# A decoder block on one core: first projections by pairs of batches, and the call lists of all five engines reordered

## The reference, cut to what matters

```python
x = x + attn(layernorm(x))                     # 8 batches, 128 tokens, 256 wide, 16 heads of 16
x = x + long_convolution(ctx, ctx, layernorm(x))
x = x + ffn(layernorm(x))                      # 4-bit weights, 2048 wide

def attn(x):
    q, k, v = x @ Wq, x @ Wk, x @ Wv
    scores = (q . k) * tril                    # masked by a product, so masked scores are 0
    return softmax(scores / 128 ** 0.5) . v @ Wo

def long_convolution(k, v, q):                 # 16 heads of 8
    kv = k_i * v_j                             # all pairs i, j of a head, per position
    y = causal_conv(kv, ssm_kernel) + kv * D
    return sum over i of y_ij * q_i

def ffn(x):
    Wg, Wu, Wd = (LUT[code] * scale for each)  # codes of 4 bits, a scale for each 32
    return (gelu(x @ Wg.T) * (x @ Wu.T)) @ Wd.T
```

## Time and profile before

| | us |
|---|---|
| median of 3 runs | 258.29 |
| lowest and highest | 256.86, 259.73 |
| span of the profiled execution | 256.6 |
| TensorE busy | 240.9 (94%) |
| VectorE busy | 158.8 (62%) |
| GpSimd busy | 138.8 (54%) |
| ScalarE busy | 127.3 (50%) |

### The profile page before, as it was taken

How to read it: one execution, slowest core, us unless ns; L and a number is a source line. 1 busy time by engine, 2 the same in 40 slices (tenths; PEclk the granted TensorE clock), 3 DMA queues, 4 the chain that set the end, 5 groups by cost and what they waited for, 6 DMA issues and landing times.

```text
span 256.6 us, 4952 instructions
## 1 busy us (share of the span) xinstructions
PE 240.9 (94%) x1840; PEld 153.7 (60%) x1840; DVE 158.8 (62%) x287; ACT 127.3 (50%) x273; POOL 138.8 (54%) x173
## 2 busy tenths in 40 slices
PE   7999999999999998876899999999999999999993
PEld 7855776566556665554445666556566566566562
DVE  1889747777798989876689976317145182322124
ACT  2345665477587777752676254325333333523230
POOL 4257563631418969796889941273453635433230
PEclk9999999999999999997999999999999999999999
DMA  6995996932030303100030000004030000000004
GB/s 192 380 353 150 164 225 201 163 66 93 3 125 4 126 4 89 42 0 0 0 125 0 0 3 1 3 0 125 0 109 17 0 3 0 0 3 0 0 0 166
DMA packets 15104, 18.81 MB, mean 73 GB/s; under 512 B 1448, under 2 KB 12776, under 8 KB 15080
## 3 DMA queue, kind: packets, MB, share of 16 engines
q1 hardware_dynamic: 15080, 18.49, 26.5%
HBM read 15.21 MB, written 3.15 MB: 72 GB/s over the span
## 4 chain that ended last, share of the span: by engine, by line
PE 80%; DVE 9%; ACT 3%; issue 3%; DMA 2%; POOL 1%; SPq 0%; DVEq 0%; ACTq 0%; POOLq 0%
PE bank L1245 39%; PE bank L1411 16%; PE bank L1301 4%; PE bank L1299 4%; PE bank L1303 3%; PE bank L1317 3%; PE bank L1482 2%; DMA X<-in_x 2%; PE bank L1369 2%; PE bank L1480 2%; ACT PT L616 2%; PE bank L1334 1%; DVE o_sb L985 1%; DVE tail L976 1%; DVE mx L960 1%
## 5 line engine op out<-in xcount | busy, mean ns | idle before, releaser
L1034 DVE SCALAR_TENSOR_TENSOR QK<-bank,QK 128x512 f32<-128x512 f32 x32 | 22.0, 689 | 60.7 <-PE bank L1245 59.7
L464 POOL TENSOR_TENSOR QK<-QK 128x512 f16<-128x512 f32 x24 | 27.7, 1156 | 56.4 <-ACT QK L645 56.4
L655 ACT ACTIVATE QK<-bank 128x512 f32<-128x512 f32 x32 | 19.0, 595 | 60.9 <-PE bank L1245 60.8
L1245 PE MATMUL bank<-xTh,Wa 128*128 128x512 f16 x128 | 40.5, 379 | 0.6 <-DVE xTl L1059 0.6
L1245 PE MATMUL bank<-xTh,Wb 128*128 128x512 f16 x128 | 40.7, 379 | 0.0
L440 POOL TENSOR_TENSOR arena<-Ys,qx 128x640 f32<-128x640 f32 x16 | 25.5, 1592 | 4.1 <-ACT qx L698 4.1
L1245 PE MATMUL bank<-xTl,Wb 128*128 128x512 f16 x64 | 24.3, 379 | 0.0
L1245 PE MATMUL bank<-xTl,Wa 128*128 128x512 f16 x64 | 24.3, 379 | 0.0
L960 DVE TENSOR_REDUCE mx<-bank 128x8 f32<-128x1024 f32 x16 | 19.5, 1220 | 7.2 <-PE bank L1334 7.2
L1411 PE MATMUL bank<-Wa,QK 128*128 128x256 f16 x192 | 23.6, 273 | 0.0
L1411 PE MATMUL bank<-Wb,QK 128*128 128x256 f16 x192 | 23.3, 273 | 0.0
(11 more groups left out here) (145 smaller groups left out, 485.7 us busy)
## 6 DMA issues: line engine op xcount, KB each, us to landing
arena<-in_codes SPq DMA_DIRECT2D x6, 384.0 KB
arena<-in_ker SPq DMA_DIRECT2D x2, 1024.0 KB, 11.5
QK<-qk_scratch SPq DMA_DIRECT2D x8, 256.0 KB, 6.0
arena<-in_ctx SPq DMA_DIRECT2D x2, 768.0 KB, 8.4
qk_scratch<-Wa SPq DMA_DIRECT2D x12, 128.0 KB, 3.4
arena<-in_gu_scale SPq DMA_DIRECT2D x6, 256.0 KB
QK<-qk_scratch SPq DMA_DIRECT2D x8, 128.0 KB, 5.9
out<-XN SPq DMA_DIRECT2D x4, 256.0 KB, 2.4
```

Of the source, the lines that this page charges most:

```text
L464: g_.tensor_tensor(il[:, u % IR], val[:, u % VR], ih[:, u % IR], ALU.subtract).then_inc(s_il, 1)
L655: s_.activation(val[:, u % VR], bank[2 * (u % 2)][:, :], ACT.Gelu_apprx_tanh, scale=1.0 / W_GAIN).then_inc(s_gel, 1)
L1034: v_.scalar_tensor_tensor(out=val[:, u % VR], in0=bank[2 * (u % 2) + 1][:, :], scalar=UP_SCALE, in1=val[:, u % VR], op0=ALU.mult, op1=ALU. ...
L1245: ins = mmul(out, a(c), w(c), start=(n == 0), stop=(n == 3 * len(chunks) - 1))
```

## The change

The first stage is written out as single calls in every engine's list, and `project_qk` of the first four batches is made in two halves of 256 columns, one for each pair of batches. Half 0 needs only `x_lo(0)` and the weight's low part; half 1 goes into the same bank beside it and signals `s_qk`. The value projections of batches 0, 1 and 2 come between the halves. The fillers are shortened. The loads of x, weights, context and Toeplitz matrices are issued in another order. All other lists keep their calls and change their order: the parts that the text speaks of are below. The waits inside a call stay, apart from those that the split needs, and the wait for all eight low parts, which moves into `convolve(0, 0)`.

```diff
-        WARM = (18, 4, 6)
+        WARM = (13, 2, 1)
...
@@ SyncE
-            load_x(0, 1)
-            load_w(0)
-            load_x(1, 1)
-            load_w(1)
-            load_x(2, 2)
-            load_w(2)
...
+            load_x(0, 1)
+            load_x(1, 1)
+            load_w(0)
+            load_skip()
+            load_w(1)
+            load_x(2, 2)
+            load_w(2)
+            load_toeplitz(0)
+            fill_minus()
+            load_wo()
+            load_ctx(0)
+            load_toeplitz(1)
+            load_ctx(1)
+            store_qk(0, 0, 0)
+            store_qk(0, 0, 1)
+            store_qk(0, 1, 0)
+            store_qk(0, 1, 1)
+            pack_qk(0, 0)
+            pack_qk(0, 1)
+            store_qk(1, 0, 0)
+            store_qk(1, 0, 1)
+            early_codes(0)
+            store_qk(1, 1, 0)
+            store_qk(1, 1, 1)
+            pack_qk(1, 0)
+            early_codes(1)
             max_rows(0)
+            pack_qk(1, 1)
             max_rows(1)
-            early_codes(1)
+            early_codes(2)
...
@@ GpSimd
             products(7)
+            decode_scale(0, 0)
             products(8)
             products(9)
+            decode_scale(0, 1)
+            max_pieces(0)
             products(10)
             products(11)
-            max_pieces(0)
-            decode_scale(0, 0)
...
             conv_products(3, 1)
-            rstd_ffn(2)
+            decode_scale(2, 1)
             conv_products(4, 0)
...
@@ ScalarE
+            weight_hi(0)
+            x_hi(0)
+            weight_hi(1)
+            x_hi(1)
+            weight_hi(2)
...
             take_ffn(2)
+            decode_hi(2)
...
@@ VectorE
+            stats_x(0)
+            stats_x(1)
+            stats_x(2)
+            stats_x(3)
+            apply_x(0)
+            apply_x(1)
+            weight_lo(0)
+            apply_x(2)
+            apply_x(3)
+            x_lo(0)
+            stats_x(4)
+            weight_lo(1)
+            stats_x(5)
+            weight_lo(2)
+            stats_x(6)
+            stats_x(7)
+            x_lo(1)
...
+            products(3)
+            products(4)
+            products(5)
+            decode_codes(0)
+            products(6)
+            products(7)
             skip_tap(8)
             skip_tap(9)
             skip_tap(10)
+            pair_max(0, 0)
...
             ffn_lo(0)
+            normalise(5)
             sum_slots(2, 0)
-            w_lo(2)
-            normalise(5)
...
+            sum_slots(3, 0)
             sum_slots(3, 1)
+            ffn_lo(2)
             normalise(7)
-            ffn_lo(2)
...
             gate_up(0)
-            sum_slots(5, 0)
+            w_lo(2)
...
@@ TensorE
+            def project_qk(n, t0, t1):
+
+                k, m = n // 2, n % 2
+                return three(bank[2 + n][:, t0 % HALF:t0 % HALF + t1 - t0],
+                             lambda c: wqkvh[:, c, k, P * m:P * m + P], lambda c: wqkvl[:, c, k, P * m:P * m + P],
+                             lambda c: xTh[:, c, t0:t1], lambda c: xTl[:, c, t0:t1], range(2))
+
+            def qk_pair(n, pr):
+
+                if pr == 0:
+                    if n == 0:
+                        keep_busy(WARM[2])
+                    pe.wait_ge(s_xtl, 1)
+                    pe.wait_ge(s_wl, n // 2 + 1)
+                    project_qk(n, 0, 256)
+                else:
+                    pe.wait_ge(s_xtl, 2)
+                    project_qk(n, 256, 512).then_inc(s_qk, 1)
...
+            transpose_x(0)
+            transpose_x(1)
+            qk_pair(0, 0)
+            qk_pair(1, 0)
+            qk_pair(2, 0)
+            qk_pair(3, 0)
+            project_v(0)
+            project_v(1)
+            qk_pair(0, 1)
+            qk_pair(1, 1)
+            qk_pair(2, 1)
+            project_v(2)
+            transpose_x(2)
+            transpose_x(3)
+            project_v(3)
+            qk_pair(3, 1)
+            project_v(4)
+            qk_half(0)
+            qk_half(1)
+            qk_half(2)
+            qk_half(3)
+            project_v(5)
+            project_v(6)
+            project_v(7)
             convolve(0, 0)
```

More of the change, by code:

```diff
@@ new lines, in load_wo, with fill_minus, store_qk @@
+            def load_wo():
+                sp.dma_start(wo[:, :, :], wo_d.rearrange("(c p) n -> p c n", p=P)).then_inc(s_w[3], 16)
+            def fill_minus():
+                sp.wait_ge(s_const, 3)
+                for g in range(2):
+                    for par in range(2):
+                        sp.dma_start(QK[64 * par + 48:64 * par + 50, g, 1],
+                                     view(minus, [[0, H // 2], [1, HALF]])).then_inc(s_minus, 16)
+            def store_qk(g, k, m):
+                sp.wait_ge(s_qkl, 4 * g + 2 * k + m + 1)
+                for part in range(2):
+                    sp.dma_start(scr[g, k, part, :, 8 * m:8 * m + 8],
+                                 nat[g][k][:, m, part, :]).then_inc(s_scr[2 * g + k], 16)
@@ new lines, in pack_qk @@
+            def pack_qk(g, k):
+                sp.wait_ge(s_scr[2 * g + k], 64)
+                for par in range(2):
+                    for first, parts, row in ((0, 2, 0), (0, 1, 32)) if k == 0 else ((0, 1, 0), (0, 2, 16)):
+                        src = scr[g, k, first:first + parts, :, par::2].rearrange("s d h t -> (s d) h t")
+                        rows = 64 * par + row
+                        sp.dma_start(QK[rows:rows + 16 * parts, g, k, :, :],
+                                     src).then_inc(s_pack[g][k], 16)
@@ L939, in skip_tap @@
                                         in1=T[:, h, 0:P], op0=ALU.mult, op1=ALU.add).then_inc(s_tdiag, 1)
-            x_lo(0)
-            x_lo(1)
-            ve.wait_ge(s_x[2], 16)
-            for b in range(4, B):
-                ln_stats(0, b)
-            weight_lo(2)
-            q_lo(0, 0)
-            ln_apply(0, 4, B)
-            ln_apply(0, 5, B)
-            q_lo(0, 1)
-            ln_apply(0, 6, B)
-            ln_apply(0, 7, B)
             def pair_max(b, p):
@@ L1282, in _, with project_v @@
+            def project_v(b):
+                pe.wait_ge(s_xtl, b // 2 + 1)
+                if b == 0:
+                    pe.wait_ge(s_wl, 3)
+                if b >= 2:
+                    pe.wait_ge(s_vs, b - 1)
+                three(bank[6 + b % 2][:, 0:D],
+                      lambda c: xTh[:, c, P * b:P * b + P], lambda c: xTl[:, c, P * b:P * b + P],
+                      lambda c: wqkvh[:, c, 2, :], lambda c: wqkvl[:, c, 2, :], range(2)).then_inc(s_v, 1)
             reader = {6: (s_vs, B), 7: (s_vs, B)}
@@ L1548, in _ @@
             attend(1, 1)
+            attend(1, 2)
             turn_max(3)
[L1550 to L1553 removed]
             attend(1, 3)
             key_scores(2, 0)
+            row_scores(5, 0)
+            turn_heads(0)
             turn_values(1)
             key_scores(2, 1)
+            project_out(0)
             attend(2, 0)
+            attend(2, 1)
+            attend(2, 2)
+            attend(2, 3)
+            key_scores(3, 0)
@@ L1639, in _ @@
             gate_and_up(2)
+            turn_query(6)
             gate_and_up(3)
+            add_cross(5)
+            gate_and_up(4)
+            down(0)
+            down(1)
             turn_query(7)
-            gate_and_up(4)
-            add_cross(5)
-            down(0)
+            turn_ffn(4)
             gate_and_up(5)
-            down(1)
-            turn_ffn(4)
             add_cross(6)
             down(2)
+            down(3)
             gate_and_up(6)
-            down(3)
+            add_cross(7)
             turn_ffn(5)
-            add_cross(7)
             gate_and_up(7)
```

540 lines of the change are left out of this document (246 added, 294 removed).

## The result

The changed kernel takes 270.49 us (269.21 to 272.00, 4 runs) where the kernel before takes 257.58 (256.74 to 259.73, 4 runs, same chip): ratio 1.047, interval 1.041 to 1.052. The prediction was 255.6 with a top of 261.5. The profiled executions have spans of 267.6 and 256.6 (the changed kernel's is one of its shorter runs, 269.28 us), so 11.0 us are to be found. Some executions of a kernel, counted as slow, last over 1.5% longer than its fastest; the ratios leave them out, and so do the times given here for e1_codes_back and e7_late_old, each the middle of two runs.

The account below looks back on a forecast made before the run. It took TensorE, busy 94% of the span, as the bound. Terms 0.0 + 1.5 + 0.6 - 5.1 + 0.3 = -2.7 took the span from 256.6 to 253.9, the median to 255.6 us; own range 253.5 to 257.5, overall 250.5 to 261.5.

Parts of the forecast that it names:

- The start: First stage: projections start at 9.3 us, convolution 0 at about 26.3, 3.0 us sooner, between 1.3 and 3.2.
- The codes: Convolution 6 waits for packed weights issued at 29.4, landed at 37.0; starts at 39.5, leaving 0.0 of the 3.0 us gained.
- The top bound, 38.6: Latest landing of codes 0: packs through at 34.8, then stores and codes one after the other, 3.8 us.
- 3.8 us: Estimate from the skill's DMA fit for the 768 KB of codes: landing at 33.2 and no stall at convolution 6.
- What queues behind it: After the codes: pair_max(0,0), score blocks and key scores wait, +1.5; low TensorE clock at convolution 6, +0.6.
- +1.5 and +0.6: Behind the codes: +1.5 us of queued waits, +0.6 (0 to 1.6) for TensorE's lowered clock after standing.
- Rival D: Slower: codes land at 38.6, TensorE stands 5 us and falls to low clock; +3.7, 262.0 us; chance 0.2.
- The middle: Attention stretch before gate_and_up: w_lo(2) leaves and swaps remove a wait; together -5.1 us, bounds -1.0 and -5.5.
- w_lo(2)'s -1.7: Attention stretch: moving w_lo(2) out of VectorE's full list saves 1.7 us, at least 1.0.
- The swaps' -3.4: End of attention: ffn_lo(2) ahead of normalise(7) removes 2.0 us of wait and 1.4 of half clock.
- After 125 us: Beside gate_and_up: w_lo(2) and decode_hi(2) join w_lo(3) where VectorE has little idle time; +0.3 us (0 to +1.0).
- The other swaps of neighbours: Remaining reorderings in the lists: counted as 0, each covered by TensorE's 94% busy share.

Follow-up runs that it names:

- e1_codes_back: Changed kernel with decode of packed weights 0 and 1, its followers, early_codes(1) and pack(1,1) back in old places; 268.3 us, ratio 1.038 to the kernel before.
- e7_late_old: e3 with the last part of four engine lists, from rstd_ffn(3) and its like on, in the old order; 262.9 us, ratio 1.023 to the kernel before.
- e12: e2 with decode_codes(0) ahead of products(6) and early_codes(0) issued behind two more stores, so convolution 6 waits for codes; 265.51 us against 256.00.
- e9: e2 with w_lo(2) moved behind gate_up(0), and decode_hi(2) and decode_scale(2,1) later as in the changed kernel; 264.35 us, ratio 1.024 to the kernel before.
- e4: Kernel before with only three swaps at the end of attention, among them ffn_lo(2) ahead of normalise(7); 257.35 us, ratio 0.997.
- e8: e2 with the three swaps of e4 added; 256.00 us, ratio 0.996 to the kernel before.
- e10: e3 with the second cross product of batches 2 to 7 over one head of sixteen, output wrong; 259.32 us, ratio 1.003 to the kernel before.
- e3: Changed kernel with one line moved: SyncE issues codes 0 ahead of the packs of group 0; 262.81 us, ratio 1.017 to the kernel before.
- e11: e2 with the second cross product of batches 2 to 7 over one head of sixteen, output wrong; 255.31 us, ratio 0.990 to the kernel before.
- e13: e2 with the changed kernel's late order on four engines, about the last 145 us; 260.14 us, ratio 1.009 to the kernel before.
- e2: Kernel before with only the new first stage, up to the first convolution, later lists in old order; 256.00 us, ratio 0.990.
- e6: e2 with 16 memsets on GpSimd ahead of rstd_cross(5), 9.6 us of work; 264.87 us, ratio 1.031 to the kernel before.

## Why the prediction was wrong, by its own steps

**The start: right.** Projections at 9.49 (9.3 forecast), convolution 0 at 26.57 (26.3). x1 landed by its place in the queue.

**The codes: the mechanism right, the size wrong.** "Of the 3.0 us nothing is left: 0.0, between -2.0 and +1.9" (the top is +1.8: 41.3 against 39.55). VectorE waits, TensorE stands ahead of convolution 6; but it starts at 43.96, not 39.5. Two terms failed. First, the codes are issued at 32.07 instead of 29.4, 2.7 us late. The prediction names both conditions of the packs, stores out and "those of queries landed", and put the second at nothing; it is the one that ended last, at 24.33, not 21.9. The sixteen engines, full at 16 to 20 in both kernels, stay full at 20 to 22 in the changed one (1.04 and 371 GB/s, before 0.38 and 121). That the loads in another order held the store is my reading; no run moves them alone. Second, from issue to landing it took 9.5 us, not 7.6. I had moved today's landing of the store behind the codes (38.4) by the packs and the new stores, and chosen 37.0. The top bound, 38.6, is 9.2 us after the issue and nearly right; it has 0.5 MB of stores and the codes at the 338 GB/s of one microsecond, counted from when the packs are through. The DMA view of 24 to 35, when stores and packs run, has 156 GB/s with the queue's packets filling 92% of the sixteen engines' time:

```profile
DMA packets 1812, 1.71 MB, mean 156 GB/s; under 512 B 138, under 2 KB 1812, under 8 KB 1812
...
q1 hardware_dynamic: 1812, 1.71, 92.0%
```

2.7 + 1.9 = 4.6, less 0.1 of a quicker decode, are the 4.5 us by which convolution 6 is late. Every packet is under 2 KB; that this is why the rate is low is my reading, no run varies it.

The Trainium skill (DMA: Bandwidth & Descriptors, section "Anatomy of one DMA"), weighed in the prediction for its 3.8 us, is further off: 9.5 us measured, from the first issue to the last landing of three loads, behind stores and packs.

**What queues behind it: under-sized.** I had +1.5 and +0.6 up to convolution 7; with the codes' 0.0 that is 2.1 in all, and 8.5 was measured. Of the missing 6.4, 4.5 are the codes. The other 1.9 are VectorE slowed beside GpSimd, which I had at its undisturbed durations: five instructions, 5.3 us instead of some 2. At those durations pair_max(0,0) would have ended by 46.4, ahead of convolution 6, and the stand of 2.52 us would not be there (an estimate from these rows). The low clock, 0.50 over 41 to 46, hides under that wait up to convolution 7; it costs behind it, where convolution 7 takes 3.5 us instead of 1.7. Rival D had the shape (5 us stand, half clock, "It decides once convolution 6 starts after about 41"), with 0.2 and a total of 262.0.

The Trainium skill (SBUF — State Buffer, section "🔬 SBUF: two separate sides") says that a VectorE instruction with two SBUF inputs and a GpSimd instruction that reads SBUF lock each other out of a shared pair of ports for the whole instruction. The rows agree: products(7) ends at 45.57, behind GpSimd's scaling (43.49 to 45.23), and the third tap at 48.59, behind the second scaling (46.84 to 48.44); with GpSimd idle in e12 a product takes 0.48.

**The middle: -5.1 forecast, -3.0 seen, and neither of its two terms gave anything by itself.** w_lo(2)'s -1.7: 0 in e9. The swaps' -3.4: 0 in e4 and e8. No run has both together without the rest, and what does give 3.0 back between convolution 7 and unit 0 is not taken apart; the wait of 2.14 us of the earlier trace rows and the half-clock stretch of the earlier trace rows, worth 1.4, are absent after.

**After 125 us: +0.3 forecast, +5.5 seen.** This is the step that I did not do. "The other swaps of neighbours in the lists I count as 0: each is covered by TensorE's 94%" was argued from TensorE's share, though project_out(0) and turn_query(0) each stand four places later in TensorE's list, and GpSimd's whole chain hangs on them. The runs showed instead that GpSimd's cross products start 38.1 us ahead of unit 0 and not 47.2, and that this lateness is worth 3.5 us (e10 against e3, with e11 for the other side). The late lists are worth 2.7 to 4.1 on a punctual GpSimd (e13). The two exceed the 4.6 that e3 loses there, so they don't add; how they share the loss stays open.

The three errors: 6.4 + 2.1 + 5.2 = 13.7, from the forecast's -2.7 to +11.0. A second way to add up, e2 with its parts: spans 253.5, and 9.7 for the wait (e12), make 263.2; the late stretch's 5.5, which is the changed kernel's own, makes 268.7, against 267.6.

## What to carry to other kernels

A reordering that puts a decode ahead of work TensorE is about to want must be timed from the landing of its load, counted from when the queue can issue it, at the rate that the same kinds of transfers show while they run together; a stand of 6.6 us in mid-kernel cost 9.5 here, and nothing gave it back. For every other engine with a chain of its own, compare its first item's lead over the point of use before and after; a share of busy time on TensorE covered nothing here. Look also at what each VectorE instruction with two inputs runs beside once the order has changed. And to find the bad part of a new order, add parts to the old kernel: taking one back out of the new kernel (e1) made new waits of 5.7, 4.8 and 2.3 us and answered nothing.

## What the runs showed of the hardware

- VectorE instructions with two inputs ran on until GpSimd's was through: a product took 1.85 us beside a scaling and a skip tap 1.64, 0.48 and 0.34 without. The other way round, GpSimd's shift took 1.84 beside VectorE's w_lo(3), 0.27 without.
- The fourth store of the queries (128 KB) landed 6.7 us after its issue at 17.64, with the sixteen engines full to 22; before, with the engines free from 20, it took 3.6 from 18.52.
- Stores to a scratch in memory and their read-back ran at 156 GB/s with the DMA engines 92% busy; a load behind them landed 9.5 us after its issue, 5.8 on a nearly idle queue.
- A stand of 6.6 to 6.9 us left TensorE's granted clock at 0.50, the 1.2 GHz level, when it resumed. The same wait of 2.1 us ahead of unit 0 left it low in the profile of before and in those of e6, e12 and e13, and not in e2's, though e6 is e2 up to there.
